# Four score banks in the last part of causal attention, and VectorE copying the gathered values there

## What is computed

```python
x = _layernorm(x + attn(x))        # 16 heads of 16 features, rotary angles, causal softmax
x = _layernorm(x + xattn(x, ctx))  # 77 context rows, all visible
x = _layernorm(x + ffn(x))         # 256 -> 1024 (gated) -> 1024 -> 1024 -> 256
# attn, per sequence:
att = jnp.einsum('bhtd,bhsd->bhts', q, k) * scale
att = jnp.where(causal, att, jnp.finfo(att.dtype).min)
att = jax.nn.softmax(att, axis=-1)
y = jnp.einsum('bhts,bhsd->bhtd', att, v)
```

## Time and profile before

| what | value |
|---|---|
| median of 3 runs | 905.83 us (905.56 to 906.2) |
| profiled execution, its own time | 905.99 us |
| its span, first to last instruction | 904.2 us |
| mean granted clock of TensorE | 0.943 |
| PE busy | 830.6 us, 92% of the span |
| ACT busy | 381.3 us, 42% |
| DVE busy | 476.8 us, 53% |

### The profile page before, as it was taken

How to read it: one execution, slowest core, us unless ns; L and a number is a source line. 1 busy time by engine, 2 the same in 40 slices (tenths; PEclk the granted TensorE clock), 3 DMA queues, 4 the chain that set the end, 5 groups by cost and what they waited for, 6 DMA issues and landing times.

```text
span 904.2 us, 14113 instructions
## 1 busy us (share of the span) xinstructions
PE 830.6 (92%) x5066; PEld 554.5 (61%) x5066; DVE 476.8 (53%) x1251; ACT 381.3 (42%) x774; POOL 321.3 (36%) x585
## 2 busy tenths in 40 slices
PE   7778988898998999999999888988989989999997
PEld 5544444334676777877777644433367667888886
DVE  4597888503776642146444778870257753117113
ACT  0566776745344411114222377766444442123210
POOL 4403325215421444435232424323343134336333
PEclk9856999959999999999999899996899999999999
DMA  9900444430000222324322034610000000000000
GB/s 300 381 1 2 176 153 141 148 120 1 1 1 2 94 94 94 116 74 160 128 107 94 25 118 163 231 52 2 1 2 1 1 2 0 1 1 24 1 1 25
DMA packets 23895, 68.70 MB, mean 76 GB/s; under 512 B 4400, under 2 KB 11568, under 8 KB 23600
## 3 DMA queue, kind: packets, MB, share of 16 engines
q1 hardware_dynamic: 23824, 67.77, 21.1%
HBM read 65.40 MB, written 13.63 MB: 87 GB/s over the span
## 4 chain that ended last, share of the span: by engine, by line
PE 76%; DVE 10%; ACT 8%; issue 3%; POOL 2%; POOLq 0%; ACTq 0%; DVEq 0%
PE bank_pair L873 26%; PE bank_pair L697 8%; PE bank_pair L679 7%; PE bank_pair L861 6%; ACT prob_s L1018 5%; PE bank_pair L791 4%; PE bank_pair L729 3%; PE bank_pair L648 3%; DVE bank_pair L1206 3%; PE bank_pair L592 3%; PE bank_pair L634 3%; DVE max_raw L1204 2%; PE bank_pair L803 2%; PE bank_pair L870 2%; PE bank_pair L780 2%
## 5 line engine op out<-in xcount | busy, mean ns | idle before, releaser
L1018 ACT ACTIVATE prob_s<-bank_pair 128x512 f32<-128x512 f32 (+3 forms) x384 | 165.7, 503 | 77.7 <-PE bank_pair L679 76.3
L1495 POOL TENSOR_TENSOR hid_lo_s<-act_raw_s,hid_hi_s 128x512 fp32r<-128x512 f32 x96 | 124.4, 1297 | 175.4 <-DVE hid_hi_s L1346 136.5
L679 PE MATMUL bank_pair<-q_t_s,k_t_s 64*128 64x512 f32 (+3 forms) x384 | 129.5, 446 | 17.3 <-ACT prob_s L1018 15.5
L1206 DVE CUSTOM_DVE_ANT_0 bank_pair<-bank_pair,causal_bf 128x128 f32<-128x128 f32 (+3 forms) x256 | 120.1, 514 | 47.6 <-PE bank_pair L648 47.1
L679 PEld LDWEIGHTS bank_pair<-q_t_s,k_t_s 64*128 64x128 f32 x384 | 62.2, 205 | 113.8 <-ACT prob_s L1018 82.0
L648 PE MATMUL bank_pair<-k_t_s,q_t_s 64*128 64x512 f32 (+3 forms) x384 | 122.1, 449 | 6.4 <-DVE max_raw L1204 3.2
L1456 POOL TENSOR_SCALAR_AFFINE_SELECT prob_s<-prob_s 128x128 f32<-128x128 f32 x256 | 72.0, 294 | 143.5 <-ACT prob_s L1018 140.8
L1346 DVE CAST hid_hi_s<-act_raw_s 128x512 fp32r<-128x512 f32 x64 | 35.9, 564 | 144.7 <-ACT act_raw_s L1085 143.8
L1085 ACT ACTIVATE act_raw_s<-bank_pair,scales 128x512 f32<-128x512 f32 x64 | 42.8, 688 | 160.2 <-PE bank_pair L873 160.2
L873 PE MATMUL bank_pair<-hid_hi_s,home_s 128*128 128x512 f32 x256 | 99.8, 390 | 0.8 <-POOL hid_lo_s L1495 0.8
L873 PE MATMUL bank_pair<-hid_lo_s,home_s 128*128 128x512 f32 x256 | 99.6, 389 | 0.0
(11 more groups left out here) (156 smaller groups left out, 1433.4 us busy)
## 6 DMA issues: line engine op xcount, KB each, us to landing
ring_s<-scratch SPq DMA_DIRECT2D x34, 512.0 KB, 3.3
home_s<-scratch SPq DMA_DIRECT2D x22, 512.0 KB, 5.9
checked_s<-in_w_ffn SPq DMA_DIRECT2D x2, 3584.0 KB, 18.2
scratch<-in_w_ffn SPq DMA_DIRECT2D x2, 2560.0 KB, 10.8
ring_moved_s<-scratch SPq DMA_DIRECT2D x10, 512.0 KB, 3.3
checked_s<-in_w_ffn SPq DMA_DIRECT2D x1, 4096.0 KB, 31.1
x_t_s<-in_x_t SPq DMA_DIRECT2D x2, 1024.0 KB, 5.4
x_tok_s<-in_x SPq DMA_DIRECT2D x2, 1024.0 KB, 9.4
```

What stands on the lines that cost most here:

```text
L679: mm(score_bank(s, j)[:, 0:CHUNK - q0], qkt(q, p, 1)[r, P * kb:P * (kb + 1)], qkt(q, p, 0)[r, CHUNK * c + q0:CHUNK * (c + 1)], start=True, ...
L1018: act.activation(prob[q][4 * (s % 2) + j][:, 0:n], score_bank(s, j)[:, 0:n], ACT.Exp, scale=SCALE).then_inc(S["exp_done"], 1)
L1206: dve.tensor_tensor_reduce(out=out[:, 0:left], in0=out[:, 0:left], in1=L["causal_bf"][:, CHUNK - left:CHUNK], scale=1.0, scalar=NEG, op0=A ...
L1495: pt(dst[1][:, m], act_raw[q][r % 3][:], dst[0][:, m].bitcast(F32), ALU.subtract).then_inc(S["f_lo"], 1)
```

## The change

From score number 132 on (`LATE_SCORE`, four scores per step, so step 33), which is behind the last step with a unit, scores go round four banks, 2, 3, 4 and 5. A score then waits for the exp of the score four before it. Score 132 itself also waits for the last reduction of a unit, which read bank 2. And the three chunks that end behind that point (chunks 5, 6 and 7, which end before steps 36, 40 and 48) have their Y copied by VectorE, not by ScalarE. All this is done once in each sequence.

```diff
+LATE_SCORE = 4 * (1 + max(max_step(p, u) for p in range(NP) for u in range(NU)))
+
+BY_VECTOR = [4 * end > LATE_SCORE for end in CHUNK_END]
...
 S_BANKS = (3, 4, 5)
+LATE_S_BANKS = (2, 3, 4, 5)
...
     def score_bank(s, j):
-        return S_BANK[(4 * s + j) % len(S_BANKS)]
+        n = 4 * s + j
+        if n >= LATE_SCORE:
+            return bank[LATE_S_BANKS[(n - LATE_SCORE) % 4]]
+        return S_BANK[n % len(S_BANKS)]
...
-            if 4 * s + j >= len(S_BANKS):
-                wait(pe, q, "exp_done", 4 * s + j - len(S_BANKS) + 1)
+            n = 4 * s + j
+            if n == LATE_SCORE:
+                wait(pe, q, "max_red", NU * NP)
+            if n > LATE_SCORE:
+                wait(pe, q, "exp_done", n - len(LATE_S_BANKS) + 1)
+            elif n >= len(S_BANKS):
+                wait(pe, q, "exp_done", n - len(S_BANKS) + 1)
...
             for n in range(2 * NG):
-                if CHUNK_END[n] == s:
+                if CHUNK_END[n] == s and not BY_VECTOR[n]:
                     y_evac(q, n)
...
+        def y_evac(q, n):
+
+            wait(dve, q, "round_mm", ROUND_AT[("y", n - 1, 0)] + 1)
+            wait(dve, q, "y_evac", n)
+            wait(dve, q, "av_done", CHUNK_END[n])
+            dve.tensor_copy(y_sb[q][:], Y[:]).then_inc(S["y_evac"], 1)
...
                 if y_step(n) == s:
                     y_norm(q, n)
+                if CHUNK_END[n] == s and BY_VECTOR[n]:
+                    y_evac(q, n)
```

More of the change, by code:

```diff
@@ L174 @@
 SHARED = (6, 2)
+assert LATE_SCORE % len(S_BANKS) == 0
 XUNIT_PAIR, XTURN_PAIR = 1, 2
```

## The result

The changed kernel takes 878.16 us (median of 4 runs, 872.73 to 878.67), the kernel before beside it 906.02 (4 runs, 905.56 to 906.7). The ratio is 0.9678, with an interval of 0.964 to 0.9717: 27.9 us faster. The forecast was 875.2, with a range of 871 to 895.

What follows compares the result with a forecast made beforehand. PE was taken as the bound, losing time to scores waiting for exps and to a clock at 0.50. 1.4 + 10.5 + 3.4 = 15.3 us per sequence, 30.6 in all, gave 875.2 us, range 871 to 895.

Steps and rivals of the forecast that it cites:

- Steps 33 to 36, 1.4 us: Attention's end, up to step 37's first score: it comes at 178.32 against 179.76, 1.4 us gained in sequence 0.
- Steps 37 to 42, 10.5 us: ScalarE's exps pace some steps; 12.7 us instead of 23.2, 10.5 gained, 4.0 of it if the level falls as before.
- the walk: Step-by-step timing from traced intervals; for the old kernel it starts the last `values` at 222.9 us, traced 223.04.
- Steps 43 to 47, 3.4 us: PE is the bound and mostly keeps the fourth score's saving: 16.7 us against 20.1, 3.4 gained.
- both falls gone, none new: The forecast case: clock at full level through both sequences' attention end, between 872 and 879 us; chance 0.47.
- The copy: Three late Y copies per sequence on VectorE, 0.66 us each, hidden; left on ScalarE, the end comes 0.2 us later.
- The reason given for the level: Ahead of the fall, work of 5.61 us goes in 4.17, making PE denser, near the stretch with units where the level stayed.
- The level falling as before: Rival: the clock falls in both sequences as before, gain 5.9 us per sequence, 894.0 us; chance 0.14.
- slower: Rival: the level falls more often, two falls beyond the present two at 9.4 us each, 912.8 us; chance 0.03.
- One fall more: Rival: one clock fall kept in one sequence or new elsewhere, costing 9.4 us, 884.6 us; chance 0.25.
- Nothing from the bank: Rival: exps set the pace everywhere, leaving only the copy, under 1 us per sequence, 904.5 us; chance 0.03.
- More than forecast: Rival: another stretch at the lower clock level goes too, about 871 us; chance 0.08.

Runs made afterwards that it cites:

- after_fill_2: Changed kernel plus idle transposes: three in step 33, two ahead of step 34's `values`, three ahead of step 36, one ahead of step 37's last score; 875.94 us.
- banks_only: Changed kernel with the four banks but ScalarE keeping all copies of Y; 878.94 us, 0.9693 of the kernel before.
- copy_only: Kernel before with its three banks, but VectorE making the three late copies of Y; 910.08 us, 1.003 of the kernel before.
- before_fill: Kernel before, three banks, plus idle transposes: three in step 33, two ahead of the fourth score in steps 33 to 41; 891.92 us, ratio 0.9837.
- six_banks: Changed kernel with six score banks in steps 33 to 41 and four from step 42; 873.73 us, 0.9631 of the kernel before.
- six_fill: Six score banks in steps 33 to 41, four from 42, plus idle transposes in two PE waits at sequence 1's start; 871.5 us, 0.9643 of kernel before.

## Why the prediction was right, and which term was off

**What bounds the kernel.** Right: all but 0.4 us of the gain lies in steps 33 to 47, from the waits behind exps and from the level of the clock.

**Steps 33 to 36, 1.4 us.** Measured 1.3 in sequence 0 and 1.6 in sequence 1. Step 37 started at 177.99, forecast 178.32, but 0.47 us of that is the head start of this trace: counted from the `values` of step 31, step 37 came at 9.44 us before and comes at 8.14 now. Step 36 came at 7.41 and comes at 6.93, so 0.48 us gained where 0.65 were taken, with bounds of 0 to 1.8 for the landing of the maxima. The DMAs were issued until 172.90 + 2.65 = 175.55, and step 36 began 1.2 us later with 0.26 us of idle time, so the landing is at most that late. The wait for the last reduction was as forecast: it costs 0.41 us in front of step 33 and is hidden, since the transpose behind it waits 0.33 us for GpSimd instead of 0.81, and step 34 comes 3.84 us behind that `values`, before 3.83.

**Steps 37 to 42, 10.5 us.** This is the term that was off. Measured 8.8: step 43 came at 192.44, 14.45 us behind step 37, where the walk had 12.7 with the level up. The forecast took both falls as gone. They weren't; each was 3.4 us long. Of the 1.75 us, 1.4 are the short fall (`after_fill_2`: 13.07) and about 0.4 are the walk's own error.

**Steps 43 to 47, 3.4 us.** Measured 3.6: 192.44 to 208.94 is 16.50 us, forecast 16.7. Third and fourth score start together or within 0.35 us in these steps.

**The sum.** 1.3 + 8.8 + 3.6 = 13.7 in sequence 0, 13.9 in sequence 1, 27.6 in all, against 27.9 between the medians; the forecast was 30.6. The miss of 3.0 us is the two short falls, 2 x 1.4, for the most part. The measured 878.16 us lies in the 872 to 879 that the prediction gave to "both falls gone, none new", and that case didn't come: each fall was cut to 3.4 us, a case it didn't have. That the time fell into this part of the range is partly luck.

**The copy.** Sized at 0.66 us, measured 0.69, from 178.03 to 178.72, with PE's transpose at 180.01 behind its scores: hidden. It was said to be worth 0.2 us per sequence; `banks_only` is 0.2 longer in one and 0.15 in the other. `copy_only` is no different from before.

**The price of the clock.** The walk had a fall at 8.0 us per sequence with three banks, and a kernel with three banks and no fall at 214.9. `before_fill` ended at 216.74 from a start 0.65 later, and 0.74 us of it are fillers in the way: 215.35 on the same footing, 7.7 us below the 223.04 with the fall. The waits' share by the walk, 214.9 - 207.7 = 7.2, is the 7.3 measured. That a fall would cost 9.4 with four banks was never measured, since no kernel with four banks had a long one.

**The reason given for the level.** The forecast said that PE would be denser ahead of the fall, as in the stretch with units, and so the level would stay. PE did become denser, 4.41 of 4.90 us and 2.77 of 3.30 (90% and 84%, before 75% and 79%), and the level fell all the same. This is the step of the reasoning that failed: denser work did not keep the level up, it went with a shorter stay. The signs that the prediction asked for came out so: third and fourth score paired in steps 34 to 47, yes, but in steps 37 and 41, where they start 0.49 us apart, and in 35, 39 and 43 (0.27 to 0.35 apart); idle time in front of them gone in 42 to 47, yes; left in 37 and 41, yes (0.49 us apart), and `six_banks` took most of it away; clock 1.00 in steps 37 to 42, no, and a stretch at 0.50 there was named as a sign that the prediction is wrong; VectorE's copy at 0.6 to 0.75 us, yes.

**The two rules.** The longest idle time ahead of the fall was 0.81 us, and in the changed kernel it was shorter than that, and the level fell in both. The rule of idle gaps in the Trainium skill, "TensorE: Matmul & The Clock Gate", section "Why this matters for your kernels", gives no fall here, so it doesn't explain these. It was used in the prediction to say that the falls would stay as they were, 894.0 us; the measured time speaks against that. The other section, "A second HAM failure mode: psum-queue depth-cycling", in which cycling through banks with brief idle times makes the level swing, fits this case better: one bank more cut the low stretch from 23.9 to 3.4 us, and six banks took it away. The trace agrees in part only, since brief idle times elsewhere bring no fall (below).

**The rivals.** The level falling as before (894.0) and slower (912.8): not so. One fall more (884.6): not as a full one; the two short ones cost 2.8 us together. Nothing from the bank (904.5): excluded by `banks_only`. More than forecast (871): not with this change; `six_fill` gets there, at 871.5.

**What stays open.** What makes the level fall just there isn't settled. `six_banks` has PE less busy than the changed kernel from 171.3 to 179.5 us (6.99 against 7.17 of 8.20), and its level stays; just ahead of the place, from 176.1 to 179.5 us, it is the busier one (3.09 against 2.87 of 3.40). But thin work alone doesn't do it: in the changed kernel PE is busy only 2.08 of 3.40 us from 206.9 to 210.3, ahead of the last `values`, and the level stays at 1.00. Busy time counts a score that runs alone as it counts two side by side, so the share is a poor measure of density; the four scores of step 37 have 2.09 us of it in the one kernel (the last of them at the lower level) and 1.11 in the other for the same work. Why a stretch at 0.50 lasts 3.4, 6.8 or 23.9 us is open too. In the windows shown of 3.4 us or less and in that of 6.8 at 0.50 PE was never idle, in those of 10.2 to 27.3 us it was busy 93% to 94%; whether that is the cause wasn't tested. And only one execution of each kernel was traced. The changed kernel's fastest run, 872.73 us, had a mean granted clock of 0.974, its other three 0.965 to 0.967, so it must have had less time at the lower level, and where isn't known.

## What to carry to other kernels

When PSUM banks come free in a part of a kernel, give them to the producer that waits for its consumer: here two engines that alternated got in each other's way once a step, and one bank more took 7.3 us of waits out of 51.7, and the better clock gave another 6.3 (7.7 less the 1.4 that a short fall keeps). Look at the granted clock in windows of a few microseconds, since a slice of 22 hides a short fall, and price a stretch at 0.50 as a term of its own. One run with idle transposes in the waits ahead of a fall tells what the clock alone is worth, provided that they stand where PE waits for something that isn't about to come; what they cost elsewhere (0.74 us here) is read from the timeline and added.

## What the runs showed of the hardware

- At the attention's end the level of TensorE's clock fell with no idle time longer than 0.81 us ahead of it, and with PE busy 74% to 90% by the records. It stayed up in a stretch where PE was busy 2.08 of 3.40 us (the changed kernel from 206.9 us). The low stretches of the attention's end were between 3.4 us (the changed kernel) and 27.3 us (`copy_only`) long.
- 42 products whose results nobody reads made the kernel before 13.9 us faster (905.81 to 891.92).
- Kernels with three banks spread over up to 13 us from run to run (900.53 to 913.33), with the mean granted clock going from 0.952 to 0.932, but `before_fill`, three banks with idle products, over 2.8 us; the kernels with four or six banks all through spread over 6 us at most. Which stretches make the difference wasn't traced.
- VectorE's copy of 128x512 floats from PSUM took 0.69 us, ScalarE's 0.63.
